# A three-hop graph network: chunks of ten groups instead of thirteen, and a sum beside every gather step of the last hop

## What is computed

```python
agg = h = relu(layernorm(x))
for _ in range(3):
    left = agg[head] @ q_w
    right = tanh((rel * agg[tail]) @ k_w)
    att = sum(left * right, axis=1)
    w = softmax of att over the edges that have the same head
    summed = segment_sum(w * rel * agg[tail], head)
    agg = summed / max(edges of the head, 1)
    agg = agg / norm(agg)
    out = out + agg + h
return x + out
```

## Time and profile before

| | |
|---|---|
| median of three runs | 2566.2 us |
| lowest, highest | 2558.34, 2572.57 us |
| the profiled execution: its own time | 2568.1 us |
| its span, first to last instruction | 2566.3 us |
| busy: DVE, POOL, PE, ACT | 1454.0, 1190.2, 1126.9, 858.7 us |
| mean granted TensorE clock, share of full | 0.652 |

### The profile page before, as it was taken

How to read it: one execution, slowest core, us unless ns; L and a number is a source line. 1 busy time by engine, 2 the same in 40 slices (tenths; PEclk the granted TensorE clock), 3 DMA queues, 4 the chain that set the end, 5 groups by cost and what they waited for, 6 DMA issues and landing times. The chain is left out here.

```text
span 2566.3 us, 24723 instructions
## 1 busy us (share of the span) xinstructions
PE 1126.9 (44%) x5196; PEld 897.6 (35%) x5196; DVE 1454.0 (57%) x7228; ACT 858.7 (33%) x2657; POOL 1190.2 (46%) x1219
## 2 busy tenths in 40 slices
PE   0112333355454545553100257688734667655430
PEld 0011222244344324453100135467623455454320
DVE  8863664453364545544339657667654644657664
ACT  3312442332333423333126433344433232222320
POOL 1034434454545354466650255552035554647666
PEclk9999655555565655556555577788567777765555
DMA  5532322221222222322225464453144644636654
GB/s 203 207 139 88 129 93 67 68 80 57 71 67 68 71 71 70 115 80 92 77 81 213 172 189 146 132 150 109 63 153 139 189 127 115 174 85 168 168 142 130
DMA packets 192463, 305.35 MB, mean 119 GB/s; under 512 B 31210, under 2 KB 113458, under 8 KB 183686
## 3 DMA queue, kind: packets, MB, share of 16 engines
q1 hardware_dynamic: 153914, 230.79, 26.9%
q0 software_dynamic: 38400, 72.99, 10.8%
HBM read 176.41 MB, written 132.67 MB: 120 GB/s over the span
## 5 line engine op out<-in xcount | busy, mean ns | idle before, releaser
L646 POOL DMA_INDIRECT tr<-in_x_dram,tidx x200 | 191.4, 957 | 508.4 <-DMA acc_d<-xr 297.1
L1574 PE MATMUL ps<-rt,wr 128*125 128x128 f32 x1200 | 266.3, 392 | 245.1 <-issue 85.0
L1503 PE MATMUL ps<-ident,rt 128*128 128x128 f32 x600 | 144.6, 385 | 449.2 <-DVE rt L1169 206.8
L646 POOL DMA_INDIRECT tr<-agg_d,tidx x200 | 191.9, 959 | 288.4 <-DMA agg_d<-rt 138.4
L1574 PEld LDWEIGHTS ps<-rt,wr 128*125 128x125 f32 x1200 | 233.0, 288 | 263.4 <-DVE wr L1094 145.5
L1381 ACT ACTIVATE sqj<-ps,invc 125x128 bf16<-125x128 f32 x600 | 212.3, 373 | 328.5 <-remote 161.1
L646 POOL DMA_INDIRECT tr<-ntab_d,tidx x200 | 193.7, 969 | 260.9 <-DVE rt L1169 196.3
L1341 ACT COPY turns<-ps 128x512 f32<-128x512 f32 x150 | 87.8, 585 | 617.1 <-PE ps L1503 351.1
L1503 PEld LDWEIGHTS ps<-ident,rt 128*128 128x128 f32 x600 | 98.0, 196 | 482.0 <-issue 248.4
L1094 DVE TENSOR_SCALAR wr<-segbc,lcol,wcol 128x125 f32<-128x125 uint8 x600 | 177.9, 349 | 153.7 <-remote 111.4
L658 POOL DMA_INDIRECT ntab_d<-rt,lidx x200 | 202.1, 1011 | 134.2 <-DVE rt L1118 75.1
(11 more groups left out here) (239 smaller groups left out, 2456.2 us busy)
## 6 DMA issues: line engine op xcount, KB each, us to landing
agg_d<-rt SPq DMA_DIRECT2D x100, 258.0 KB
xr<-agg_d SPq DMA_DIRECT2D x100, 258.0 KB
relr<-rel_d SPq DMA_DIRECT2D x100, 256.0 KB
ntab_d<-rt SPq DMA_DIRECT2D x10, 2519.5 KB
acc_d<-xr SPq DMA_DIRECT2D x50, 258.0 KB
rel_d<-relr SPq DMA_DIRECT2D x50, 256.0 KB
hr<-acc_d SPq DMA_DIRECT2D x50, 256.0 KB
hr<-agg_d SPq DMA_DIRECT2D x50, 256.0 KB
```

The costliest lines, as they stand in the source:

```text
L646: G.indirect_dma_start(out=row, out_offset=None, in_=table[:, :], in_offset=bass.IndirectOffsetOnAxis(ap=idx[:, n:n + 1], axis=0)).then_in ...
L1503: ins = T.transpose(ps[B_TR][:, t, :], rt[:, g * GT + t, 0:D], ident[:, :])
L1574: ins = T.matmul(ps[B_T + j % 2][0:R, t, :], wr[:, (j % 2) * GT + t, 0:R], rt[:, j * GT + t, 0:D], start=True, stop=True)
```

## The change

Five chunks of ten groups replace four of 13, 13, 13 and 11. All units of hop 0 are then pairs (25). The stages of hops 1 and 2 get a third place in a step, behind the scaling on DVE, so a chunk's stages end after parts of four steps; PE takes the parts 40 or 20 at a time. In hop 2 a group is summed in every step: with the earlier first carries, hops 1 and 2 now sum groups 0 to 33 in steps 18 to 51, and hop 0 sums 15 in its loop. FILL becomes [5, 3, 3]. One chunk's late pair moves: seven early chunks, and late ones at steps 1, 7 and 13 only. The negated masks `gfn` and `gbn`, made once for all chunks, become `gneg`, made for each chunk at stage 0 behind the request to PE.

```diff
-K = 4
-GC = [0, 13, 26, 39, NG]
+K = 5
+GC = [0, 10, 20, 30, 40, NG]
...
-NDE = 5
+NDE = 7
...
-LATE_AT = [1, 7, 13, 19]
+LATE_AT = [1, 7, 13]
...
-PLACES = [3, 2, 2]
+PLACES = [3, 3, 3]
...
-PARTS = [26, 13, 13]
-EVERY = [1, 1, 2]
+PARTS = [40, 20, 20]
+EVERY = [1, 1, 1]
...
-FILL, HOLD = 5, 2
+FILL, HOLD = [5, 3, 3], 2
...
-    return sums_left(h)[FILL:len(sums_left(h)) - HOLD]
+    return sums_left(h)[FILL[h]:len(sums_left(h)) - HOLD]
...
-    return sums_left(h)[i:i + 1] if i < FILL else range(0)
+    return sums_left(h)[i:i + 1] if i < FILL[h] else range(0)
...
-        gf = sb("gf", [Q, K, R], BF16)
-        gb = sb("gb", [Q, K, R], BF16)
-        gfn = sb("gfn", [Q, K, R], BF16)
-        gbn = sb("gbn", [Q, K, R], BF16)
+        gfb = sb("gfb", [Q, 2, K, R], BF16)
+        gf, gb = gfb[:, 0, :, :], gfb[:, 1, :, :]
+        gneg = sb("gneg", [Q, 2, R], BF16)
...
-            ch.note(V.tensor_scalar(gfn[:, :, :], gf[:, :, :], BIG, -BIG, ALU.mult, ALU.add))
-            ch(V.tensor_scalar(gbn[:, :, :], gb[:, :, :], BIG, -BIG, ALU.mult, ALU.add))
...
-                marks = (gf, gb) if add else (gfn, gbn)
+                marks = (gf[0:n, b, :], gb[0:n, b, :]) if add else (gneg[0:n, 0, :], gneg[0:n, 1, :])
...
                     ask()
+                    ch.note(V.tensor_scalar(gneg[0:n, :, :], gfb[0:n, :, b, :], BIG, -BIG, ALU.mult, ALU.add))
                 elif stage == 1:
...
                             scaled(h, j)
+                    if h > 0:
+                        softmax(h, *stage_at(h, s, 2))
...
                             turned(h, s)
-                        if stage_at(h, s, 0)[1] == 3:
-                            exps(h, stage_at(h, s, 0)[0])
                         if 1 <= s <= NG:
                             tanh(h, s - 1)
...
                             dense(c, range(DC // 2, DC))
+                        if stage_at(h, s, 2)[1] == 3:
+                            exps(h, stage_at(h, s, 2)[0])
                     for j in sums_at(h, s - 1):
...
                         softmax(*stage_at(h, s, 1))
+                        softmax(*stage_at(h, s, 2))
                     parts(h, *parts_at(h, s))
```

More of the change, by code:

```diff
@@ L284, in gnn_kernel @@
         LS, LL, LF, LB, LSP = range(5)
-        lx = [chunks_of(28 + 2 * k, P) for k in range(5)]
-        seg0, seg0f, seg0n = (chunks_of(38 + 2 * k, R) for k in range(3))
+        lx = [chunks_of(29 + 3 * k, P) for k in range(5)]
+        seg0, seg0f, seg0n = (chunks_of(83 + 3 * k, R) for k in range(3))
         erow = flat[0:1, 8 * SC:8 * SC + 5 * NT].rearrange("p (k n) -> p k n", k=5)
@@ L947, in terms @@
                 n, part = CT[b], slice(TC[b], TC[b + 1])
-                marks = (gf, gb) if add else (gfn, gbn)
+                marks = (gf[0:n, b, :], gb[0:n, b, :]) if add else (gneg[0:n, 0, :], gneg[0:n, 1, :])
                 lines = (G_, GN, WGF, WGB) if add else (GNEG, GNNEG, WGFN, WGBN)
                 return (n, (ALU.mult, ALU.add) if add else (ALU.add, ALU.max), 0.0 if add else LOWEST,
-                        [m[0:n, b, :] for m in marks], [rows[:, k, part] for k in lines])
+                        marks, [rows[:, k, part] for k in lines])
             def within_tiles(add, b, state):
```

## The result

The changed kernel takes 2665.3 us (median of 4 runs, 2663.92 to 2675.62) against 2569.4 us for the kernel before in the same session: ratio 1.0388, 95% interval 1.0344 to 1.0432. It is **3.9% slower**. The forecast was 2545 us with a range up to 2600. The profiled execution took 2675.62 us and spans 2673.9, 107.6 us more than before.

The account below looks back on a forecast made before the run. No engine was full (DVE busiest, 57%); time was lost in waits. Hop 2 -26, hop 1 -4, hop 0 +8 and mask +1 gave -21 us: 2547, or 2545 us as shown median, eight-in-ten range 2498 to 2600.

Parts of the forecast that it names:

- the floor: Hop 2's end: POOL scatters almost without waiting for DVE, 279 us from first scatter to end; 26 us earlier overall.
- Rival 5: Hop 2's tail: POOL, never waiting, holds DVE, ACT and PE up; no change, 2566 us; chance 0.11.
- The step pace: Hop 2's steps 24 to 44: summing and scaling a group each step takes 8.65 us a step, +24 us.
- late chunk and weights: Hop 2's loop: dropping step 19's late chunk gives -13 us, six groups' weights in steps 18 to 23 add +5.
- The fifth chunk: Loops of hops 1 and 2: +7 us for another carry and 2 for eight more stages, +9 each.
- The third place: Hop 2's loop: stage 3 and ACT's exponential behind the scaling, hidden by DVE's longer step; uncovered some 2 us a chunk.
- Hop 0, +8: Hop 0: two more early chunks +8, extra chunk and counts +6, shorter tail -6; bounds -15 to +25 us.
- Removal of a late chunk, -13: Loops of hops 1 and 2: one late chunk fewer saves twice an excess of 6.5 us, -13 each.
- Rival 2: Hop 2, steps 18 to 44: DVE's added work paid in full, +66, and 10 in hop 1; 2596 us; chance 0.18.
- Rival 3: Hop 2's loop: transfers bind it, 1.54 MB a step taking 9.7 us at 159 GB/s; 2572 us; chance 0.08.
- Rival 1: Hop 2's loop: even steps shrink unexplained waits, first scatter at 2240 instead of 2261; 2524 us; chance 0.18.
- Rival 4: Hop 2: DVE's scaling and POOL's gathers exclude each other, lengthening gathers by 53 us; 2555 us; chance 0.03.

Follow-up runs that it names:

- before_every1_2: Kernel before with only hop 2 summing a group every step, still four chunks, on the chip like the first: ratio 0.9993.
- after_parts10_early5: Changed kernel with parts of 10 a step in hops 1 and 2, five early chunks, late ones at steps 1, 6, 11, 16: 1.0409 of before.
- The best version: Kernel before with hop 2 summing every step, parts of 9, scatters mixed with gathers from group 38: 0.9837 on a faster chip, 0.981 on one like the first.

## Why the prediction was wrong

Forecast and measured shift, in us: hop 0 +8 and +16, hop 1 -4 and +42, hop 2 to the first scatter +25 and +44, from the first scatter to the end -52 and +6. So of the 129 us between the forecast span and the measured one, 57 lie in the floor, 46 in hop 1 and 19 in hop 2's loop.

**The floor, -26 us with the later first scatter: failed on this chip.** The step was "DVE in time ... by 18 us", with 12 us for each of eight steps beside uninterrupted scatters. I had the mechanism and took its size from a window of 15 us that held little more than one step. In the run of 96 DMAs PE's slow pace set in only after 20 us, and the four steps took 153 us, 38 each. From first scatter to end are 336 us (2673.9 - 2337.5), as before (330.7), and the sum in each step alone leaves 329. Rival 5, "the tail gives it back", was the true course of hop 2's end; at 308 us (16 per step) it was still priced 28 us too low. On the faster chips the floor held within 3 us (276 to 279 us in the kernels with a sum in each step and the scatters unmoved), so its arithmetic was sound; the premise about DVE was not. That the hold-up is a matter of the chip I could not know from one trace.

**The step pace, +24: nearly twice too dear.** The sum in each step alone makes steps 24 to 44 of hop 2 take 161.5 us (`before_every1_2`), 13 more than before and not 24. **With late chunk and weights, -8:** without fifth chunk, portions and third place, product 44 comes 334 us after hop 2's first product, 9 more than before, where these terms give 16. That they come near in the sum is partly luck: the late chunk that left hop 2 shows as 3 us there (334 against 337), not 13. In hop 1 it is nearer: 332 against 344.

**The fifth chunk, +9 in each hop: failed, together with the size of the portions, which had no price in the loops.** "Two steps about a carry take 20.8 us where two usual ones take 14.0" was read from portions of 13. In hop 1 of the changed kernel the carry's step is 22 to 23 us by itself, and the stages' step (groups 33, 43) 19; about 10 us of the latter are a late update of PE's semaphore, which a faster chip does not have. Hop 1 came out at +42 instead of -4, and hop 2's loop at +44 instead of +25. The tail of hop 1 gave back 22 us, more than the 11 forecast. The chunk and the size of its portions can hardly be priced apart: each further chunk brings the waits behind a portion once more. On the faster chips smaller portions give back 28 us, four chunks 21, both 38; on a chip like the first neither was undone alone. I had spoken of portions only for the last chunk's forty parts.

**The third place: "some 2 us a chunk" without cover.** Not measurable alone; undone as the last of three it closed the gap. It remains open whether it weighs so only beside portions of 13, or whether the chip matters.

**Hop 0, +8: 16 measured**, within its stated bounds. The two early chunks alone are 12 us of it by `after_parts10_early5`, near the 8 given for them. **Removal of a late chunk, -13**, had the right sign: putting one back cost 15 us in hop 1's loop, though at a closer spacing.

**The mask, +1**: not tested alone. **Rival 2** had the right side, and in hop 2's loop half of the cause. To product 44 DVE works 61 us more than before (168 and 229 us) and the stretch is 44 longer, between the forecast's 25 and this rival's 66. But with the sum in each step alone, 39 us more work lengthen it by only 12; so it is not DVE's work as such that was paid, and half the loss came before hop 2, where this rival had 10 us. **Rival 3** had a small share at most: in the loop's second stretch DVE waits for the tables 11.4 us in eight waits, and 167 GB/s is less than the 226 seen before. **Rival 1** fell: product 44 did not come earlier in any version on a chip like the first.

**Rival 4** fell by the trace. Scatters average 1.027 us against a median of 0.982, 0.045 us each, and the gathers behind group 24's product 0.989 us against 0.970 before; by this rival they would have lengthened by 53 us in all. The Trainium skill (SBUF — State Buffer, "Who interferes with whom") speaks of an exclusive lock for the whole instruction; this trace shows no lengthening of that size, and no run here tells whether issuing an indirect DMA falls under that rule. What stopped was DVE, PE and ACT, for much longer than any instruction lasts.

Of the marks I gave, "hop 1 within 10 us of its 444 us" (it took 486, 1465.1 to 1951) and "scatters with waits for DVE under 15 us" failed first, and hop 2's steps 24 to 44 took 9.0 us each instead of 8.6; "long waits of scatters for DVE after 2400 mean rival 5" pointed the right way.

## What to carry to other kernels

Here PE worked off whatever was queued in one lump and in order (40 matmuls, 5.4 us): the size of a portion that is slipped between the steps of a chain is paid at the waits of that chain. So try more, smaller portions, and price a new chunk by its carry's step as it will be, not as it was. Before moving work out of a tail so that one engine may issue DMAs without pause, look in the trace for a long enough run of that kind, and count what the others got done in it; a window with one step in it tells little. And a floor worked out for one engine says nothing unless the engines that feed it keep their pace under it.

## What was not expected of the hardware

- In a run of 96 indirect DMAs from POOL, PE started, after some 20 us, a matmul every 2.80 us where 14 otherwise pass in 2.95 us, and DVE and ACT started nothing for 76.9 us.
- Many waits that the profile calls "remote" are waits for PE whose semaphore update is recorded late: up to 42 us after the matmul's modelled end, 77 to 100 such waits of over 2 us in each trace of the slower kind of chip, none in those of the faster. Whether the matmul ends late or only its update is slow, and why PE's pace falls, is open.
- It depends on the chip: the same program had DVE busy for 19 of 100 us on one and 64 of 79 us on another, at nearly the same rate of DMAs. The kernel before took 2569 and 2597 us on two chips and 1966 to 1972 us on four; hop 0's loop alone took 798 us (222 to 1020) and 523 us (194 to 717) in one and the same program.
- The change was a loss on both kinds, 1.039 and 1.046 to 1.048, and on both it was made before the first scatter; on the first, besides, the gain hoped for behind it did not come. The best version was a gain on both, 0.981 and 0.984.
